# Two attention layers in one program: where one batch hands over to the next, the last group of keys runs beside the next batch's first scores, and rounds hold 12 or 16 tiles

## The reference

```python
# x: (4, 2048, 256)
def attn(x):                                    # 16 heads of 16
    q, k, v = split((x @ w_in.T + b_in).reshape(b, l, 16, -1), 3)
    att = softmax(einsum('blhd,bmhd->blmh', q, k) / sqrt(16), axis=2)
    opt = einsum('blmh,blhd->blhd', att, v)     # the row's own v, times the sum over its row
    return opt.reshape(b, l, d) @ w_out.T + b_out
def ffn(x):                                     # 4 of 16 heads of 64, chosen per batch
    dist = softmax(mean(x @ Wr + br, axis=1))
    idx = sort(top_k(dist, 4))
    Q, K, V = the projections of x by the chosen heads
    S = softmax(Q @ K.T / sqrt(64))
    return (S @ V).reshape(b, s, 256) @ Wo + bo
x = layernorm(x + attn(x))
x = layernorm(x + ffn(x))
```

## Time and profile before

| | |
|---|---|
| median of 3 runs | 4088.38 us |
| the profiled execution | 4086.6 us, its span 4084.8 us |
| busy | PE 89%, DVE 80%, ACT 76%, POOL 41% |
| mean granted clock of PE | 0.887 of 2.4 GHz |
| last tile of batch 0, 1, 2, 3 (DVE) | 756.9, 1661.3, 2576.1, 3490.9 us |
| first score of batch 0, 1, 2, 3 (DVE) | 891.9, 1806.5, 2721.2, 3591.7 us |

### The profile page before, as it was taken

The page is one execution under the profiler, slowest core; times in us unless marked ns, Lnnn a source line. Parts: engine busy times, 40 slices in busy tenths (PEclk is TensorE's granted clock), DMA queues, the critical chain, the costliest instruction groups (busy, mean ns, idle before and its releaser), DMA issues.

```text
span 4084.8 us, 41654 instructions
## 1 busy us (share of the span) xinstructions
PE 3616.2 (89%) x13992; PEld 1329.7 (33%) x13992; DVE 3287.2 (80%) x3352; ACT 3098.1 (76%) x5069; POOL 1662.8 (41%) x1115
## 2 busy tenths in 40 slices
PE   7888888778999999788999999788999999599997
PEld 3233223223333333323333332323333322343443
DVE  7888888988989898888989898888989898543442
ACT  5888888886888889786888889786888889423333
POOL 3122332100445555400445545401445545437776
PEclk7777777678999999878999999778999999799998
DMA  5122221110000000210000000210000000100000
GB/s 159 67 75 67 83 75 62 57 45 16 16 16 19 21 21 26 67 38 16 16 16 19 26 16 26 73 33 16 16 16 25 21 16 19 53 9 1 11 11 11
DMA packets 117192, 142.62 MB, mean 35 GB/s; under 512 B 33394, under 2 KB 100466, under 8 KB 116978
## 3 DMA queue, kind: packets, MB, share of 16 engines
q1 hardware_dynamic: 116978, 139.95, 11.0%
HBM read 89.55 MB, written 50.33 MB: 34 GB/s over the span
## 4 chain that ended last, share of the span: by engine, by line
PE 47%; DVE 29%; ACT 17%; issue 5%; POOL 2%; SPq 1%; DMA 0%; POOLq 0%; DVEq 0%; ACTq 0%
DVE nmax L1083 18%; ACT ps L920 14%; PE ps L796 8%; PE ps L886 8%; PE ps L858 7%; PE ps L761 7%; PE ps L873 7%; DVE smax L1162 6%; PE ps L775 6%; POOL facc L720 2%; PE ps L876 2%; PE ps L769 1%; PE ps L894 1%; ACT probs L990 1%; DVE st L1062 1%
## 5 line engine op out<-in xcount | busy, mean ns | idle before, releaser
L920 ACT ACTIVATE ps<-ps,nmax 128x1024 f32<-128x1024 f32 x2048 | 2233.0, 1094 | 388.4 <-DVE nmax L1083 365.6
L1083 DVE TENSOR_REDUCE nmax<-ps 128x1 f32<-128x1024 f32 x2048 | 2379.4, 1216 | 135.2 <-PE ps L796 122.5
L796 PE MATMUL ps<-stack 96*128 96x512 bf16 x4096 | 1350.6, 436 | 237.0 <-ACT ps L920 149.4
L720 POOL TENSOR_TENSOR facc<-facc,probs 128x1024 f32<-128x1024 f32 x448 | 1051.2, 2346 | 550.9 <-ACT probs L990 528.8
L1162 DVE TENSOR_REDUCE smax<-ps 128x2 f32<-128x1024 f32 x512 | 616.5, 1220 | 261.3 <-PE ps L858 260.9
L796 PEld LDWEIGHTS ps<-stack 96*128 96x128 bf16 x4096 | 298.2, 102 | 1411.0 <-ACT ps L920 939.2
L990 ACT ACTIVATE probs<-ps 128x1024 f32<-128x1024 f32 x512 | 524.0, 1024 | 229.1 <-PE ps L876 227.8
L858 PE MATMUL ps<-fk,fq 64*128 64x512 f32 x2048 | 571.0, 650 | 41.4 <-ACT ps L920 38.1
L873 PE MATMUL ps<-fq,fk 64*128 64x512 f32 x2048 | 545.7, 609 | 29.0 <-ACT ps L920 27.9
L886 PE MATMUL ps<-probs,vals 128*64 128x512 f32 x2048 | 506.9, 608 | 5.0 <-ACT probs L990 4.5
L920 ACT ACTIVATION_READ_ACCUMULATOR ps<-ps,nmax 128x1 f32 x2048 | 417.0, 204 | 0.0
(11 more groups left out here) (117 smaller groups left out, 1985.5 us busy)
## 6 DMA issues: line engine op xcount, KB each, us to landing
stack<-qk_levels SPq DMA_DIRECT2D x768, 64.0 KB, 2.2
qk_levels<-fk SPq DMA_DIRECT2D x64, 384.0 KB, 2.6
probs<-in_L_attn_x SPq DMA_DIRECT2D x16, 512.0 KB, 3.8
res<-in_L_attn_x SPq DMA_DIRECT2D x16, 512.0 KB, 4.0
v_rows<-vals SPq DMA_DIRECT2D x16, 512.0 KB, 2.6
vrows<-v_rows SPq DMA_DIRECT2D x16, 512.0 KB, 3.4
x_rows<-y SPq DMA_DIRECT2D x16, 512.0 KB, 2.9
res<-x_rows SPq DMA_DIRECT2D x16, 512.0 KB, 3.9
```

The source lines that it names most:

```text
L720: pool.tensor_tensor(total, total, probs[:, slot, :], ALU.add).then_inc(facc_ready, 1)
L796: last = pe.matmul(bank(banks[i]), stack[0:SK, hd % 2, 0, t * P:(t + 1) * P], stack[0:SK, hd % 2, 1, col:col + CH], start=True, stop=True)
L920: act.activation(src, src, ACT.Exp, bias=nmax[:, b % 2, half, t, hd:hd + 1], scale=-1.0, accum_out=esum[:, b % 2, half, t, hd:hd + 1]).the ...
L1083: dve.tensor_reduce(nmax[:, b % 2, half, t, hd:hd + 1], two_banks(banks), AX.XY, ALU.min).then_inc(min_ready, 1)
```

## The change

The last group's `T` and `V` of a batch become part of the next batch's first rounds; the rounds of all batches form one sequence of `B * 32 + 4`. `AHEAD` becomes 20. Lead rounds stay for batch 0 alone (and, in form, for batch 3, where T and V of batch 2's last group get spots within the seam). A round has 16 tiles while more are left than 12 a round would place, else 12; batch 3's have none. `D`, `R` and `FO` of the last group follow in the next batch. Its transposed output needs another place, since `x1T` is being rewritten: `foT(3)` is `oT`. The projections of the second pair's keys and of the values get a list of their own, `late`, and their waits are for the step that frees their piece, not for the whole batch. The planner's costs are set nearer to measured ones.

```diff
-AHEAD = 70
-ROUND = "TSSTAASTAASTAAAVVAAVAVAA"
-LEAD = "SAAAASAAAASAAAASAAAA"
+AHEAD = 20
+EARLY = 8
+ROUNDS = {0: "TSSTSTSTVVVV", 12: "AASTAASTSATASTAAAVVAAVAV", 16: "STAASTAASTAASTAAAVAVAAVAAVAA"}
+LEAD = "SAAAASAAAASAAAASAAAATTTTVVVV"
...
+    for r in range(B * rounds + behind):
+        b, k = divmod(r, rounds)
+        if r < behind or b == B - 1 and k < behind:
+            spots = LEAD
+        elif b + 1 < B:
+            spots = ROUNDS[16 if A_TILES - given[b] > 12 * (rounds - k) - EARLY else 12]
+        else:
+            spots = ROUNDS[0]
+        take = {"S": r * BURST, "T": r * BURST - STEPS, "V": r * BURST - STEPS}
...
+            if kind != "S" and b == B - 1 and k < behind:
+                spot = b + near * (k + i / len(spots)) / behind
...
-    norms = [(k, b, c) for b in range(B) for k in ("OP", "FO") for c in range(NCH)]
+    norms = []
+    for b in range(B):
+        norms += [("OP", b, c) for c in range(NCH)] + [("FO", b - 1, NCH - 1)] * (b > 0)
+        norms += [("FO", b, c) for c in range(NCH - 1)]
...
-            fill(("A", b, j), 0.46, 2, [sp("LS", b, j // HEAD_TILES)] if j % HEAD_TILES == 0 else [], act("A", b, j))
-            unit(dve("A", b, j), 1.155, [pe("A", b, j)])
+            fill(("A", b, j), 0.437, 2, [sp("LS", b, j // HEAD_TILES)] if j % HEAD_TILES == 0 else [], act("A", b, j))
+            unit(dve("A", b, j), 1.135, [pe("A", b, j)])
...
-        foT = x1T
+        def foT(c):
+            return oT[:, :, :] if c + 1 == NCH else x1T[:, :, c * CH:(c + 1) * CH]
+
...
+                    if b:
+                        act.wait_ge(filled, fill_no["T", b - 1, GROUPS - PAIRS + p, c * TPC + TPC - 1])
...
-                        dve.wait_ge(pv_done, step_no(b - 1, GROUPS - 1, STEPS - 1))
+                        dve.wait_ge(pv_done, step_no(b - 1, GROUPS - 1, c * TPC + TPC - 1))
...
+                    if c + 1 == NCH and b + 1 < B:
+                        dve.wait_ge(filled, fill_no["OP", b + 1, NCH - 1])
```

More of the change, by code:

```diff
@@ L73, in work_lists, with spot_of @@
     tiles += place([("A", 0, j) for j in range(A_TILES)], -1, 1)
+    near = AHEAD / A_TILES
+    rounds = GROUPS * STEPS // BURST
+    behind = STEPS // BURST
+    def spot_of(r, part):
+        b, k = divmod(r, rounds)
+        if b == B:
+            return B + (k + part) / rounds
+        return b + near + (1 - near) * (k + part) / rounds
     for b in range(B):
-        near = AHEAD / A_TILES
         if b + 1 < B:
@@ L111, in work_lists @@
-        if b + 1 < B:
-            tiles += [(b + 0.9999, ("A", b + 1, j)) for j in range(given, A_TILES)]
-        main += [(b + 0.9999, ("D", b, GROUPS - 1)), (b + 0.9999, ("R", b, GROUPS - 1))]
-        main.append((b + 0.9999, ("FO", b, NCH - 1)))
+        later = [u for c in range(NCH) for u in (("FK", b, 1, c), ("FV", b, c))] + [("FQ", b, 1, 0)]
+        late += [(spot_of(b * rounds + behind * (i + 1) / len(later), 0.0), u) for i, u in enumerate(later)]
+        main += [(spot_of(b * rounds + behind * g - behind / 2, 0), ("FQ", b, g % PAIRS, g // PAIRS)) for g in range(2, GROUPS)]
@@ new lines, in work_lists @@
+    given = [AHEAD] * B
+    for r in range(B * rounds + behind):
+        b, k = divmod(r, rounds)
+        if r < behind or b == B - 1 and k < behind:
[5 more added lines that the diff above has]
+        take = {"S": r * BURST, "T": r * BURST - STEPS, "V": r * BURST - STEPS}
+        for i, kind in enumerate(spots):
+            spot = spot_of(r, i / len(spots))
+            if kind == "A":
+                if b + 1 < B and given[b] < A_TILES:
+                    tiles.append((spot, ("A", b + 1, given[b])))
+                    given[b] += 1
+                continue
+            n = take[kind]
+            take[kind] += 1
+            if not 0 <= n < B * GROUPS * STEPS:
+                continue
+            at, step = divmod(n, STEPS)
+            if kind != "S" and b == B - 1 and k < behind:
+                spot = b + near * (k + i / len(spots)) / behind
+            unit = (kind, at // GROUPS, at % GROUPS, step)
+            (products if kind == "V" else scores).append((spot, unit))
+            if kind == "T" and step == 0:
+                main.append((spot, ("M",) + unit[1:3]))
+            if kind == "V" and at:
+                was = ((at - 1) // GROUPS, (at - 1) % GROUPS)
+                main += [(spot, ("D",) + was)] * (step == 4) + [(spot, ("R",) + was)] * (step == 8)
+                main += [(spot, ("FO", was[0], was[1] // PAIRS))] * (step == 12 and was[1] % PAIRS == 1)
@@ L115, in work_lists @@
+    for b in range(B - 1):
+        tiles += [(b + 0.9999, ("A", b + 1, j)) for j in range(given[b], A_TILES)]
+    main += [(B + 0.99, ("D", B - 1, GROUPS - 1)), (B + 0.99, ("R", B - 1, GROUPS - 1)), (B + 0.99, ("FO", B - 1, NCH - 1))]
+    for units in (late, scores, products, tiles):
+        units.sort(key=lambda entry: entry[0])
     main.sort(key=lambda entry: entry[0])
-    return [main, scores, products, inputs, tiles]
+    return [main, scores, products, inputs, tiles, late]
 def plan():
@@ L235, in plan @@
             fill(("R", b, g), 0.75, 1, [pool("D", b, g)], dve("R", b, g))
[L236 removed]
+            free = [pe("OP", b + 1, NCH - 1)] if b + 1 < B and c + 1 == NCH else []
+            unit(dve("R", b, g), 0.68, [pe("R", b, g), pool("V", b, g, BURSTS - 1)] + free)
     for i, (k, b, c) in enumerate(norms):
```

91 lines of the change are left out of this document (38 added, 53 removed).

## The result

The changed kernel takes **3984.6 us** (median of 4 runs, 3982.7 to 3985.1) against 4088.4 (4 runs, 4086.7 to 4088.7): a ratio of **0.9746**, 95% interval 0.9729 to 0.9763, faster by 2.5%. The forecast was 3975 in a range of 3900 to 4065. The profiled execution took 3985.1 us, its span is 3983.3.

What follows compares the result with a forecast made beforehand. No engine alone bounds it: TensorE limits the main rounds, ScalarE the last four; VectorE becomes longest after the change. Middle cycles -82, first cycle -34, last seam and batch 3 +4: -112 on 4086.6 gives 3975 us, range 3900 to 4065.

Steps and rivals of the forecast that it cites:

- 727.4 / 0.95 = 766: Main rounds of batches 1 and 2: 727.4 us of VectorE work at a 95% share take 766 us.
- the slower rival: Main rounds: TensorE's granted clock falls below 0.85; at 0.80 the kernel takes about 4235 us; chance 0.05.
- Forecast 108: Seams of batches 1 and 2: 13 + 76 + 21 x 0.9 = 108 us each, bounds 95 and 125.
- 0.9 us for each tile between: Middle seams: each tile between transposes and first score, outside the wait for weights, lengthens the seam by 0.9 us.
- the 76 of the bare chain: Middle seams: transposes to first score take 76.0 us without tiles, read from the last seam before the change.
- -34: First cycle, seam, lead and rest together: 870 us against 904.3, a gain of 34 us.
- the rest is 584.5 + (27 + 23) x 1.135 = 641.2 of VectorE: First cycle after seam and lead: 641.2 us of VectorE work, at 95% taking 675 us.
- -3: Last seam: 100.8 - 13 + 10 = 98 us, slightly shorter than before.
- The chain loses its 13: Last seam: transposes start some 13 us earlier, since the last group's denominators, reciprocals and output chunk run later.
- I charge 10 us: Last seam: 10 us for the last group's TensorE work between chain links, including normalisations slowed beside GpSimd.
- up to 19 us: Last seam: longer by up to 19 us if each of eight short VectorE products meets a GpSimd instruction.
- +6.5: Batch 3's scores to the end: moved denominators, reciprocals and output chunk add 6.5 us to 493.1.

Runs made afterwards that it cites:

- Experiments 10 and 11: Changed kernel with 20 (10) or 12 (11) tiles, not 16, in each of the first four rounds of batches 1 and 2: 3988.2 and 3994.5 us.
- Experiment 7: Changed kernel with 70 tiles of the next batch in a seam (AHEAD = 70), not 20: 4000.9 us.
- experiment 2: Changed kernel with batch 2's last keys as rows and products beside batch 3's first scores, not in the last seam: 3985.5 us.
- experiment 1: Changed kernel with GpSimd's 15 additions for batch 2's last group cut to 64 of 1024 columns, leaving its denominators wrong: 3957.1 us.

## Why the prediction was right, and where it was not

**What bounds, and the main rounds: right.** A round of 16 tiles was to take 24.9 us; the group of four above took 97.6, 24.4 each. VectorE's share was to be 95%: it is 96.0% in that group, 95.7% in the rest of the first cycle, and 93.1% over the rounds of batch 1 (721.8 of 775.2), because the first four are at 79%. I applied one share to all 32, and "727.4 / 0.95 = 766" was too short: they took 775 to 777. That is the mis-sized term in both middle cycles, +9 and +11 us. Experiments 10 and 11 show that no slack was to be had by moving tiles. The clock, on which the slower rival hung, was 0.98 to 0.99 in the rounds. The Trainium skill's case of the clock swinging through bank waits (TensorE: Matmul & The Clock Gate, "A second HAM failure mode: psum-queue depth-cycling") did not show in them.

**Seams of batches 1 and 2: right in size, for mixed reasons.** Forecast 108, measured 105.5 and 105.6. Transposes start at 1619.3, 17.6 us after the last tile, not 13: the joining takes longer than before, since GpSimd's additions meet it too. The row of TensorE's timeline after, and those of the joining in VectorE's:

```profile
1619.25 1.94 PE L804 MATMUL ps<-ident,vrows 128*128 128x128 f32 x8 [3.42 <-POOL vrows L718]
```

```profile
1605.52 2.28 DVE L1072 TENSOR_TENSOR oT<-nmax 128x256 f32<-128x256 f32 x1
1607.83 2.72 DVE L1074 TENSOR_TENSOR oT<-oT,nmax 128x512 f32<-128x512 f32 x1
...
1612.32 2.52 DVE L1083 TENSOR_TENSOR oT<-oT 128x256 f32<-128x256 f32 x1
```

The first cycle, which has no such additions there, had 0.42, 0.69 and 0.42 us for these. From the transposes on it took 88 us instead of the forecast 95, so 0.9 us for each tile between, or the 76 of the bare chain, was too much. The two misses, 4.6 too little and 7 too much, nearly cancel. Experiment 7 shows the better way to count: VectorE's idle time in the seam is 26 to 31 us with either number of tiles.

**First cycle: too careful, -34 against -56.** The step that failed is "the rest is 584.5 + (27 + 23) x 1.135 = 641.2 of VectorE". It kept in the cycle all that VectorE did there before. But at a cycle's end the last group now stays open: residual and row statistics of one output chunk, its product, and three scores move over the boundary. The cycle has 784.8 us of VectorE instead of 794.3 (the three windows of the earlier trace rows from 757.0 on), and the rest 628.6 instead of 641.2; by 0.95 that is 13 us, the higher share gives 5, the seam 7, and the lead takes 3 back (87.4 against 84). In the middle cycles what leaves at the end has come in at the start, and nothing shows.

**Last seam: wrong, +22.4 against -3.** Two terms. "The chain loses its 13": bare as in experiment 2 it is 95.9 long, so it loses 4.9. Its transposes start 17.5 us after the last tile, before 24.8, so they come 7 us sooner and not 13; and VectorE waits 4.6 us for a store, which before did not stand there. And "I charge 10 us", for TensorE between the links and one or two meetings with GpSimd: together they cost 27.3 (123.2 against 95.9), of which experiment 1 gives 1.9 to TensorE and up to 25.4 to the meetings. So -4.9 + 27.3 make the 22.4. I had taken the number of meetings from a seam in which GpSimd has 29 us of work, and the change gives it 76. The prediction quotes the rule that says it: the Trainium skill (SBUF — State Buffer, "Who interferes with whom") has a VectorE instruction with two SBUF inputs and a GpSimd one that reads SBUF wait for each other to the end, and I worked out up to 19 us by it and left it out of the sum. The count behind the 19 was short as well: the seam has twelve such products (L678, L680 and L684, four each), not eight. VectorE's busy time grew by 17.0 us (67.1 against 50.2 with short additions), and the chain by 8 more. The same section of the Trainium skill counts `tensor_scalar` among the instructions that can take the shared port, on conditions for their operands, and this trace agrees: the row scalings, 1.38 or 5.5 us for four, are such and have one tensor as input, and they are the largest part of the 17.0, 7.4 us (15.7 against 8.3). I had priced only the products of two operands.

**The end: +1.6 against +6.5.** Denominators, reciprocals and output chunk of the group left open now stand there too, and TensorE is busy 7.2 us more (463.1 against 455.9); that the rest was hidden is my reading, no experiment took them out.

The misses nearly cancel: 22 us in the first cycle, 5 at the end and 4 before the first cycle for, 25 in the last seam and 16 in the middle cycles against; the total came out 10 us off, which is better than its terms. That closeness is luck.

## What to carry to other kernels

- When work moves into idle time of one engine, list what it puts on *every* engine there, and price the meetings by what will run after the change, not by the rows of before. Here 15 GpSimd additions filled its idle time, and up to 25 us of VectorE's chain went with them; handing them to VectorE, which is in that chain itself, gave 10 to 21 back.
- In a software pipeline count the gain by cycle, and ask at each boundary what now crosses it. The first and the last cycle are the ones that don't balance.
- An engine at 79% beside one at 95% need not be room for work. Add a known number of units and read the cost of one: 1.16 us here, more than in the tight rounds (0.97).
- Before a difference of two seams is put down to an edit, look where the two traces first part. Here 2.3 us of it stood there before the edited instructions began.
